# The delta stage of a state-space layer in 512-column pieces, with another split of its passes over the engines

## The chip, the cores and the metric

The kernel runs on one core of a Trainium2 chip. The metric is the device time of one execution in microseconds; smaller is better. Engines are called as in the profile: PE (TensorE), ACT (ScalarE), DVE (VectorE), POOL (GpSimd) and SP (SyncE, which issues most DMAs). Each has its own instruction queue, runs it in order and meets the others through semaphores.

## The reference, cut to what matters

The program is a state-space layer (norm, delta stage, scan, merge), then attention and a mixture of experts. Only the delta stage and its weights are touched. It works on 8 units (2 images times 4 branches of 64 channels), each 48x48 = 2304 positions long, with 128 inner channels:

```
x  = silu(conv3x3_depthwise(x @ in_W) + conv_b)         # 64 -> 128 channels
xs = [x0, x1, reversed x0, reversed x1]                 # x1 is x with rows and columns swapped
dts, B, C = split(einsum('bkdl,kcd->bkcl', xs, x_proj_W), [4, 16, 16])
delta = softplus(einsum('bkrl,kdr->bkdl', dts, dt_W) + dt_b)
# the scan then wants delta, delta * u, B and C for each of the 4 directions
```

## The kernel before, in words

`setup_phase` loads the weights with SP, multiplies dt_W with the first four rows of x_proj_W into one 128x128 matrix per direction (`w_eff`, L142), transposes the rest (`w_bc`, L147, L171) and makes the convolution's matrices `w_pair` and `w_one` (L166, L167). `norm_phase` writes the normalised input to `xn` in memory. Each phase ends for all engines before the next begins.

`delta_phase` loops over pairs of units (`Fori`, L389, L434, L500). A unit has 12 steps of 768 columns: 4 directions (0, 2, 1, 3) by 3 chunks. In a step:

- PE makes two 384-column products with `w_eff` in fp32 into `ps_a` (L376), one 384-column piece of B and C into `ps_b` (L380), and, on every second step, six matmuls of a convolution block of the *next* unit into `ps_c` (L361 with 128 rows, L362 with 64). Before the first unit all six of its blocks stand alone.
- ACT takes Abs and Relu of `ps_a` plus the bias (L415, L416), then Exp of minus Abs back into `ps_a` (L418). After three steps it switches its table and takes three logarithms (L402).
- DVE makes `dm` = (1 + e) - 1 (L477), copies `ps_b` out (L472), takes `ps_a` - `dm` (L448), and after three steps adds the logarithm (L455) and the Relu (L461), which gives delta.
- POOL multiplies delta with x (L518), turns x for directions 1 and 3 (L520), and makes `b_lo` (L508), the rest of B after its fp32r rounding `b_hi` (ACT, L407).
- SP stores `dd` (delta and delta*u together, L335), B and C (L320), `b_hi` and `b_lo` (L323) and x (L329), and loads images (L315) into `pad`, whose rows are 50 long, so that a row arrives in 192-byte runs.

`ps_a` has three buffers, and PE may start step n only when delta of step n-3 is written (`delta_done`, L373). Since DVE finishes three steps together, the engines work in bursts of three steps.

Of the kernel before, what the change touches and what calls it, by code (L numbers as in the profile page):

```python
# [22 lines left out]
K = 4  # L23
# [5 lines left out]
PAIRS = 2  # L29
SOFT = (4, 12)  # L30
# [41 lines left out]
def setup_phase(nc, P, w, keep):  # L72

    with ExitStack() as ctx:
        s = Space(nc, ctx, "setup")
        dts_rows = s.sb("dts_rows", [R, K, D])
        dtw_t = s.sb("dtw_t", [R, K, D])
        bc_rows = s.sb("bc_rows", [2 * N, K, D])
# [18 lines left out]
        loads.append((keep["dt_b"][:, :], w["dt_b"].rearrange("k d -> d k")))  # L97
# [13 lines left out]
        @block.sync  # L111
        def _(sp):
            for dst, src in loads:
                sp.dma_start(dst, src, allow_slow_non_contiguous=True).then_inc(loaded, 16)

        @block.gpsimd
        def _(pool):
            pool.memset(keep["ident"][:, :], 0.0).then_inc(ones_set, 1)
# [18 lines left out]
        @block.tensor  # L137
        def _(pe):
            pe.wait_ge(loaded, 16 * n_loads)

            for k in range(K):
                mm = pe.matmul(ps_w[:, k, 0:D], dts_rows[:, k, :], dtw_t[:, k, :], start=True, stop=True)  # L142
            mm.then_inc(weff_ps, 1)
            pe.wait_ge(ident_set, 1)
            pe.wait_ge(dve_done, 1)
            for k in range(K):
                mm = pe.transpose(ps_w[:, k, 256:256 + 2 * N], bc_rows[:, k, :], keep["ident"][0:2 * N, 0:2 * N])  # L147
            mm.then_inc(bc_ps, 1)

        @block.scalar  # L150
        def _(act):
            act.wait_ge(loaded, 16 * n_loads)
            act.activation(a_exp[:, :, :], a_log[:, :, :], ACT.Exp).then_inc(exp_done, 1)

        @block.vector
        def _(dve):
            dve.wait_ge(weff_ps, 1)
            dve.tensor_copy(keep["w_eff"][:, :, :], ps_w[:, :, 0:D]).then_inc(dve_done, 1)
            dve.wait_ge(exp_done, 1)
            dve.wait_ge(pool_set, 4)  # L160
            dve.tensor_scalar(keep["a_neg"][:, :, :], a_exp[:, :, :], -1.0, None, ALU.mult).then_inc(a_done, 1)

            for dy in range(3):
                for half in range(2):
                    p = slice(64 * half, 64 * half + 64)
                    dve.tensor_tensor(keep["w_pair"][p, dy, :], in_w2[p, :], conv_taps[p, :, 3 * dy + half], ALU.mult)  # L166
                dve.tensor_tensor(keep["w_one"][:, dy, :], in_w2[0:64, :], conv_taps[0:64, :, 3 * dy + 2], ALU.mult)  # L167
            dve.tensor_reduce(keep["d_sum"][:, :], ds4[:, :], AX.X, ALU.add)
            dve.wait_ge(bc_ps, 1)
            for r in range(2):  # L170
                dve.tensor_copy(keep["w_bc"][:, :, :].rearrange("d p (b r n) -> d r p b n", b=2, r=2)[:, r],  # L171
                                ps_w[:, 2 * r:2 * r + 2, 256:256 + 2 * N].rearrange("d p (b n) -> d p b n", b=2))
# [99 lines left out]
def delta_phase(nc, P, keep):  # L272
# [4 lines left out]
    with ExitStack() as ctx:  # L277
        s = Space(nc, ctx, "delta")

        pad = s.sb("pad", [128, 2, H + 2, W + 2])  # L280
        xs = [s.sb(f"xs{i}", [128, L]) for i in range(2)]
        xt = [s.sb(f"xt{i}", [128, L]) for i in range(2)]
        ring = lambda name: [s.sb(f"{name}{i}", [128, WC]) for i in range(3)]
        mag, pos, lg, dm = ring("mag"), ring("pos"), ring("lg"), ring("dm")
        dd = [s.sb(f"dd{i}", [128, 2, WC]) for i in range(3)]
        bc = [s.sb(f"bc{i}", [4 * N, L]) for i in range(2)]
        b_hi = [s.sb(f"b_hi{i}", [2 * N, L], F32R) for i in range(2)]
        b_lo = [s.sb(f"b_lo{i}", [2 * N, L], F32R) for i in range(2)]
        ps_a = [s.ps(f"ps_a{i}", [128, 2, 512]) for i in range(3)]
        ps_b = s.ps("ps_b", [4 * N, 512])  # L290
        ps_c = s.ps("ps_c", [128, 512])
        cleared, x_done, xt_done = s.sem("cleared"), s.sem("x_done"), s.sem("xt_done")
        img_here = [s.sem("img_here0"), s.sem("img_here1")]
        xs_out = [s.sem("xs_out0"), s.sem("xs_out1")]
        a_full, b_full, b_taken, c_full, c_taken = (s.sem(x) for x in ("a_full", "b_full", "b_taken", "c_full", "c_taken"))
        mag_done, ex_done, lg_done, hi_done = (s.sem(x) for x in ("mag_done", "ex_done", "lg_done", "hi_done"))
        dm_done, co_done, sm_done, delta_done = (s.sem(x) for x in ("dm_done", "co_done", "sm_done", "delta_done"))
        du_done, lo_done = s.sem("du_done"), s.sem("lo_done")
        dd_out = [s.sem(f"dd_out{i}") for i in range(3)]
        bc_out = [s.sem(f"bc_out{i}") for i in range(2)]  # L300
        block = ctx.enter_context(nc.Block())
        UP = U // 2
        Q = STEPS
        src = P["xn"].rearrange("b (r c) l -> (b r) c l", r=BR)
        halves = lambda x: x[:, :].rearrange("p (a b) -> p a b", a=2)
        order = [(p + 2 * r, c) for p in range(PAIRS) for r in range(2) for c in range(NCH)]
        bcd = P["bc"].rearrange("u (r p) b n l -> u p b r n l", p=PAIRS)
        cutd = P["cut"].rearrange("u (r p) a n l -> u p a r n l", p=PAIRS)

        @block.sync  # L310
        def _(sp):
            def load_image(n, k):
                img = src[n].rearrange("c (h w) -> c h w", h=H)
                for half in range(2):
                    sp.dma_start(pad[64 * half:64 * half + 64, k, 1:H + 1, 1 - half:W + 1 - half], img).then_inc(img_here[k], 16)  # L315

            def keep_bc(u, unit, p):
                sp.wait_ge(b_taken, unit * Q + 6 * p + 6 + 1)
                for b in range(2):
                    sp.dma_start(bcd[u, p, b], bc[p][32 * b:32 * b + 32, :]).then_inc(bc_out[p], 16)  # L320
                sp.wait_ge(lo_done, unit * PAIRS + p + 1)
                for a, cut in enumerate((b_hi, b_lo)):
                    sp.dma_start(cutd[u, p, a], cut[p][:, :].bitcast(F32)).then_inc(bc_out[p], 16)  # L323

            def pair(i, last):
                for k in range(2):
                    unit = i * 2 + k
                    sp.wait_ge(x_done, unit + 1)
                    sp.dma_start(P["xs"][i * 2 + k], xs[k][:, :]).then_inc(xs_out[k], 16)  # L329
                    if not last:  # L330
                        load_image(i * 2 + (k + 2), k)
                    for q, (d, c) in enumerate(order):
                        t = k * Q + q
# [1543 lines left out]
```

## Time and profile before

| | us |
|---|---|
| median of 3 runs (lowest to highest) | 6581.43 (6579.79 to 6591.75) |
| the profiled execution: its own time, its span | 6577.67, 6575.9 |
| setup and norm | 0 to 95.8 |
| delta stage, first to last engine instruction | 95.8 to 955.9 |
| first instruction of the scan | 988.75 |
| busy over the span: PE, DVE, POOL, ACT | 5383.8, 4385.1, 4109.4, 3873.2 |

Positions are microseconds from the start of the span. The share of busy time over the whole span says little of this change, since the scan (from 988.75) has two thirds of it; the stretch between 95.8 and 988.75 is what counts. TensorE's clock has two levels here, 1.2 GHz (0.50) and 2.4 GHz (1.00), and a stretch shows their mean.

### The profile page before, as it was taken

Reading aid. Unit: us, or ns where it says so; the run is one execution under the profiler, and the core shown is the slowest. Engines: PE = TensorE matmul, PEld = TensorE weight load, DVE = VectorE, ACT = ScalarE, POOL = GpSimd, SP = SyncE. Lnnn points to the kernel's source line nnn. Section 1 sums busy time; section 2 is a strip of 40 time slices with the busy share of each in tenths; the row PEclk is TensorE's granted clock in tenths of the full one; section 3 lists DMA queues with packets and bytes.
Section 4 is the critical chain, followed back from the end, with each engine's and each line's share of the span. In section 5 each row is a group of like instructions: output and inputs, shape, how many; then the busy total and the mean of one; then the engine's idle time right before and its main releaser. Section 6 shows DMA issues by size and latency. Waiting matters only on the chain. (4 is left out here: it accounts for less than half of the span.)

```text
span 6575.9 us, 86273 instructions
## 1 busy us (share of the span) xinstructions
PE 5383.8 (82%) x22548; PEld 3529.8 (54%) x22548; DVE 4385.1 (67%) x4337; ACT 3873.2 (59%) x7966; POOL 4109.4 (62%) x2729
## 2 busy tenths in 40 slices
PE   5767648999989899898998999955589999966994
PEld 2222215555555555555555555522269999944773
DVE  2455548999999999999999999967331211153332
ACT  2565557788778788778887888844532222232232
POOL 0233338999989999899998999942014444402441
PEclk7788879999999999999999999977789999975997
DMA  3344337777777777777777777765200000012213
GB/s 79 116 148 140 141 131 233 249 249 244 250 234 248 243 247 245 238 247 244 247 248 239 249 244 248 246 210 176 97 22 0 0 0 0 0 50 88 78 59 107
DMA packets 432423, 1073.25 MB, mean 163 GB/s; under 512 B 97545, under 2 KB 140586, under 8 KB 427386
## 3 DMA queue, kind: packets, MB, share of 16 engines
q1 hardware_dynamic: 420570, 1043.06, 48.9%
q0 software_dynamic: 7584, 20.72, 1.0%
q10 hardware_dynamic: 3840, 4.72, 0.3%
q8 instruction: 151, 2.47, 0.2%
q14 instruction: 278, 2.28, 0.1%
HBM read 883.38 MB, written 184.94 MB: 162 GB/s over the span
## 5 line engine op out<-in xcount | busy, mean ns | idle before, releaser
L852 POOL TENSOR_TENSOR scan_hc<-scan_h,scan_c_rep 128x768 f32<-128x768 f32 x1536 | 2745.3, 1828 | 282.1 <-PE scan_ps_y L683 220.2
L683 PE MATMUL scan_ps_y<-scan_hc,keep_ident 128*128 128x512 f32 (+1 forms) x6144 | 2221.9, 489 | 21.6 <-ACT scan_y L718 21.6
L817 DVE TENSOR_TENSOR_SCAN scan_h<-scan_da,scan_h,scan_ps_p 128x768 f32<-128x768 f32 x896 | 1573.4, 1795 | 0.0
L683 PEld LDWEIGHTS scan_ps_y<-scan_hc,keep_ident 128*128 128x128 f32 x6144 | 1070.2, 191 | 824.6 <-issue 740.6
L774 ACT ACTIVATE scan_da<-scan_dd,layer_a_neg 128x768 f32<-128x768 f32 x1344 | 1208.9, 925 | 195.9 <-DVE scan_h L817 190.3
L735 ACT ACTIVATE scan_warm<-scan_du_t 128x128 f32<-128x128 f32 x4032 | 1243.0, 388 | 2.5 <-PE scan_ps_p L674 1.9
L1194 POOL TENSOR_TENSOR attn_e_lo<-attn_e,attn_e_hi 128x384 fp32r<-128x384 f32 x432 | 438.2, 1014 | 773.1 <-DVE attn_e_hi L1185 773.1
L817 DVE TENSOR_TENSOR_SCAN scan_h<-scan_da,scan_ps_p 128x768 f32<-128x768 f32 x448 | 760.7, 1733 | 2.0 <-ACT scan_da L774 2.0
L796 DVE TENSOR_TENSOR scan_ps_p<-scan_ps_p,scan_dd 128x768 f32<-128x768 f32 x672 | 634.6, 944 | 137.2 <-PE scan_ps_p L666 135.7
L1185 DVE CAST attn_e_hi<-attn_e 128x384 fp32r<-128x384 f32 x432 | 165.3, 383 | 713.6 <-ACT attn_e L1173 713.6
L674 PE MATMUL scan_ps_p<-keep_ident,scan_warm 128*128 128x128 f32 x4032 | 580.5, 281 | 71.5 <-DVE scan_h L817 67.2
L1173 ACT ACTIVATE attn_e<-attn_ps_s 128x384 f32<-128x384 f32 x432 | 212.7, 492 | 692.4 <-PE attn_ps_s L69 692.4
L666 PE MATMUL scan_ps_p<-scan_cut,layer_b_sel 128*128 128x512 f32 x1344 | 434.7, 405 | 159.5 <-DVE scan_h L817 146.9
L674 PEld LDWEIGHTS scan_ps_p<-keep_ident,scan_warm 128*128 128x128 f32 x4032 | 444.9, 142 | 215.3 <-issue 138.1
L666 PEld LDWEIGHTS scan_ps_p<-scan_cut,layer_b_sel 128*128 128x128 f32 x1344 | 218.7, 190 | 341.2 <-DVE scan_h L817 301.6
L846 POOL TENSOR_TENSOR scan_bu<-scan_dd,scan_b_rep 128x768 f32<-128x768 f32 x192 | 350.3, 1825 | 0.0
L518 POOL TENSOR_TENSOR delta_dd<-delta_dd,delta_xs 128x768 f32<-128x768 f32 x48 | 86.1, 1810 | 402.7 <-DVE delta_dd L461 402.5
L67 PE MATMUL attn_ps_s<-f_hi,f_lo 128*128 x864 | 293.2, 339 | 2.1 <-DVE attn_t_lo L1181 2.1
L67 PE MATMUL attn_ps_o<-attn_e_hi,attn_t_lo 128*128 128x384 f32 x864 | 291.4, 337 | 3.8 <-POOL attn_e_lo L1194 3.8
L69 PE MATMUL attn_ps_s<-f_hi 128*128 x864 | 293.1, 339 | 0.0
L68 PE MATMUL attn_ps_s<-f_lo,f_hi 128*128 x864 | 291.6, 338 | 0.0
L69 PE MATMUL attn_ps_o<-attn_e_hi,attn_t_hi 128*128 128x384 f32 x864 | 291.5, 337 | 0.0
(279 smaller groups left out, 7483.2 us busy)
## 6 DMA issues: line engine op xcount, KB each, us to landing
scan_c_rep<-bc_dram SPq DMA_DIRECT2D x1536, 384.0 KB, 4.2
dd_dram<-delta_dd SPq DMA_DIRECT2D x96, 768.0 KB, 3.4
scan_dd<-dd_dram SPq DMA_DIRECT2D x96, 768.0 KB, 5.6
scan_b_rep<-bc_dram SPq DMA_DIRECT2D x192, 384.0 KB, 4.8
y_dram<-scan_y SPq DMA_DIRECT2D x96, 384.0 KB, 4.5
merge_y<-y_dram SPq DMA_DIRECT2D x32, 1152.0 KB, 10.6
delta_pad<-xn_dram SPq DMA_DIRECT2D x16, 576.0 KB, 27.3
xs_dram<-delta_xs SPq DMA_DIRECT2D x8, 1152.0 KB, 25.4
```

The source lines that it names most:

```text
L67: pe.matmul(out, wl, xh, start=start, stop=False)
L69: return pe.matmul(out, wh, xh, start=False, stop=stop)
L666: mm = pe.matmul(ps_p[place(t) % PR][:, lo:hi], keep["b_sel"][:, n, :], cut[st % 2][:, lo:hi], start=True, stop=True)
L674: mm = pe.transpose(ps_p[place(t) % PR][:, b * 128:b * 128 + 128], warm[w % WR][:, b, :], keep["ident"][:, :])
L683: mm = pe.matmul(ps_y[:, lo:hi], keep["ident"][:, :], hc[t % HR][:, lo:hi], start=n == 0, stop=n == N - 1)
L735: last = act.activation(warm[w % WR][:, b, :], du_t[st % 2][:, b * 128:b * 128 + 128], ACT.Identity, scale=du_t[st % 2][:, at:at + 1])
L774: act.activation(dst, dd[st % 2][:, 0, :], ACT.Exp, scale=keep["a_neg"][:, k, n:n + 1]).then_inc(ex_done, 1)
L796: dve.tensor_tensor(x, x, dd[st % 2][:, 1, :], ALU.mult).then_inc(mult_done, 1)
L817: dve.tensor_tensor_scan(view(h[n]), view(x), view(y), start, ALU.mult, ALU.add).then_inc(scan_done, 1)
L846: pool.tensor_tensor(bu[f % SR][:, :], dd[st % 2][:, 1, :], b_rep[f % SR][:, :], ALU.mult).then_inc(bu_done, 1)
L852: pool.tensor_tensor(hc[t % HR][:, :], h[t % N][:, :], c_rep[t % CR][:, :], ALU.mult).then_inc(hc_done, 1)
L1194: pool.tensor_tensor(e_lo[j % 4][:, :], e[j % 4][:, :], e_hi[j % 4][:, :].bitcast(F32), ALU.subtract).then_inc(lo_done, 1)
```

## The change

Everything up to the end of the norm keeps its order, but the weights differ: `w_eff` and `dt_b` are gone. Instead `w_dt` holds dt_W transposed as fp32r with the bias as one more row, and `w_dt_lo` what the rounding left of it; nine small loads (`late`) bring them, after the others.

The delta stage is written out without loops, as 16 rounds. A round is two directions of one unit, 0 and 2 (from `xs`) or 1 and 3 (from `xt`), 4608 columns in nine pieces of 512:

- `project` makes, for the next round, dts, B and C together (96 rows, 384 columns a block, six blocks a round). ACT rounds 40 rows into `cut` (and copies even blocks to `bc`), DVE writes the rest of the rounding into `cut` rows 64 to 103 (and copies odd blocks). Only then may PE start the next block.
- `expand` makes a piece of delta's argument out of `cut` with two fp32r matmuls (four in the piece across both directions).
- ACT takes Abs (without bias) and Exp into a second PSUM buffer `ps_e`; three logarithms of 1536 columns a round, in place in `du`.
- DVE makes `dm` in `du`, `ps_e` - `dm` in `de`, then max(`ps_a`, 0) + `de` in one pass; in the next round it adds the logarithm, 768 columns at a time, from SBUF to SBUF (`add_log`).
- POOL only multiplies with x and turns x.
- A convolution block is issued in halves of three matmuls. Its matrices are ordered by dx, so that images lie in `img` without a border inside a row (2304 columns in one run) and the outer taps have 47 of 48 columns. Three buffers of `xs` let it run up to two units ahead.
- SP stores delta and delta*u with two DMAs a chunk.

The stage's diff, cut to its core:

```diff
-        pad = s.sb("pad", [128, 2, H + 2, W + 2])
-        ps_a = [s.ps(f"ps_a{i}", [128, 2, 512]) for i in range(3)]
+        img = [s.sb(f"img{i}", [128, L + 2 * W]) for i in range(2)]
+        cut = [s.sb(f"cut{i}", [STACK, L], F32R) for i in range(2)]
+        de = [s.sb(f"de{i}", [128, 2 * L]) for i in range(2)]
+        du = [s.sb(f"du{i}", [128, 2 * L]) for i in range(2)]
+        ps_a = [s.ps(f"ps_a{i}", [128, PIECE]) for i in range(3)]
+        ps_e = [s.ps(f"ps_e{i}", [128, PIECE]) for i in range(3)]
+        SLOTS = (1, 2, 4, 5, 7, 8)
...
+            # SP
+            for g in range(G):
+                if g: store_dd(g - 1)
+                if g + 1 < G: store_bc(g + 1)
+                if p == 0 and u + 1 < U:
+                    store_xs(u + 1)
+                    if u + 3 < U: load_image(u + 3)
...
+            # PE
+            def project(g, b):
+                if m:
+                    pe.wait_ge(lo_done, m)
+                    pe.wait_ge(even_taken, (m + 1) // 2)
+                pe.matmul(ps_b[0:6 * N, 0:TT], keep["w_bc"][:, p, :], x[:, b * TT:b * TT + TT], ...).then_inc(b_full, 1)
+            def expand(g, i):
+                n = g * IG + i
+                if n >= 3: pe.wait_ge(v_done, n - 2)
+                for r, at, a, b in spans(i):
+                    pe.matmul(ps_a[n % 3][:, a:b], keep["w_dt"][:, d, :], cut[g % 2][:, at:at + b - a], ...)
+                    mm = pe.matmul(ps_a[n % 3][:, a:b], keep["w_dt_lo"][:, d, :], cut[g % 2][0:64, at:at + b - a], ...)
+                mm.then_inc(a_full, 1)
+            for t in range(TPI): convolve(0, t, 0, 6)
+            for t in range(3): convolve(1, t, 0, 6)
+            for b in range(TPI): project(0, b)
+            for g in range(G):
+                for i in range(IG):
+                    expand(g, i)
+                    if proj_block(g, i): project(*proj_block(g, i))
+                    if conv_block(g, i) and i % 3 < 2:
+                        convolve(*conv_block(g, i), 3 * (i % 3), 3 * (i % 3) + 3)
...
+            # ACT
+            def log(g, r):
+                act.wait_ge(co_done, IG * g + 3 * r + 3)
+                act.activation(x, x, ACT.Ln, bias=1.0).then_inc(ln_done, 1)
+            for g in range(G):
+                for i in range(IG):
+                    magnitude(n + 1)
+                    act.wait_ge(mag_done, n + 1)
+                    if n >= 3: act.wait_ge(co_done, n - 2)
+                    act.activation(ps_e[n % 3][:, :], mag[n % 3][:, :], ACT.Exp, scale=-1.0).then_inc(ex_done, 1)
+                    if i + 1 < IG and proj_block(g, i + 1): take_block(*proj_block(g, i + 1))
+                for r in range(LOGS): log(g, r)
+                if g % PAIRS == 0 and g // PAIRS + 1 < U: silu(g // PAIRS + 1)
...
+            # DVE
+            def add_log(g, j):
+                dve.wait_ge(ln_done, LOGS * g + j // 2 + 1)
+                dve.tensor_tensor(de[g % 2][:, at], de[g % 2][:, at], du[g % 2][:, at], ALU.add).then_inc(de_done, 1)
+                    if i == 0 and g >= 2: dve.wait_ge(dd_out[g % 2], 32 * CG * (g // 2))
+                    dve.wait_ge(ex_done, n + 1)
+                    dve.tensor_scalar(du[g % 2][:, at], ps_e[n % 3][:, :], 1.0, -1.0, ALU.add, ALU.add).then_inc(dm_done, 1)
+                    if i + 1 < IG and proj_block(g, i + 1): take_block(*proj_block(g, i + 1))
+                    dve.wait_ge(dm_done, n + 1)
+                    dve.tensor_tensor(de[g % 2][:, at], ps_e[n % 3][:, :], du[g % 2][:, at], ALU.subtract).then_inc(co_done, 1)
+                    if conv_block(g, i) and i % 3 == 1: take_conv(*conv_block(g, i))
+                    dve.wait_ge(co_done, n + 1)
+                    dve.scalar_tensor_tensor(de[g % 2][:, at], ps_a[n % 3][:, :], 0.0, de[g % 2][:, at], ALU.max, ALU.add).then_inc(v_done, 1)
+                    if g and 0 < i <= CG: add_log(g - 1, i - 1)
```

The order of DVE's instructions before, three steps of a unit (L477 makes `dm`, L472 copies `ps_b`, L448 corrects, L455 adds the logarithm, L461 the Relu):

```order
L477 TENSOR_SCALAR delta_dm<-delta_ps_a 128x768
L472 COPY delta_bc<-delta_ps_b 64x384
L448 TENSOR_TENSOR delta_ps_a<-delta_ps_a,delta_dm 128x2x384
L455 TENSOR_TENSOR delta_ps_a<-delta_ps_a,delta_lg 128x2x384 x2
L460 ISA
L461 TENSOR_TENSOR delta_dd<-delta_ps_a,delta_pos 128x768
L455 TENSOR_TENSOR delta_ps_a<-delta_ps_a,delta_lg 128x2x384
L461 TENSOR_TENSOR delta_dd<-delta_ps_a,delta_pos 128x768 x2
```

And now, pieces 1 to 3 of a round (L547 `dm`, L517 and L519 the next round's block, L551 the correction, L511 a convolution block, L555 max and add, L525 the logarithm of the round before):

```order
L547 TENSOR_SCALAR delta_du<-delta_ps_e 128x512
L517 COPY delta_bc<-delta_ps_b 96x384
L519 TENSOR_TENSOR delta_cut<-delta_ps_b,delta_cut 40x384
L551 TENSOR_TENSOR delta_de<-delta_ps_e,delta_du 128x512
L511 COPY delta_xs<-delta_ps_c 128x384
L555 SCALAR_TENSOR_TENSOR delta_de<-delta_ps_a,delta_de 128x512
L525 TENSOR_TENSOR delta_de<-delta_de,delta_du 128x768
L547 TENSOR_SCALAR delta_du<-delta_ps_e 128x512
L551 TENSOR_TENSOR delta_de<-delta_ps_e,delta_du 128x512
L555 SCALAR_TENSOR_TENSOR delta_de<-delta_ps_a,delta_de 128x512
L525 TENSOR_TENSOR delta_de<-delta_de,delta_du 128x768
```

The additions no longer come in a group after three steps: each `ps_a` buffer is given back within its own piece, and the logarithm is added a round later, out of SBUF.

ACT's order before, where it leaves one group of three steps for the next:

```order
L418 ACTIVATE delta_ps_a<-delta_mag 128x2x384
L402 ACT_TABLE_LOAD
L402 ACTIVATE delta_lg<-delta_dm 128x768 x3
L414 REGISTER_ALU
L415 ACTIVATE delta_mag<-delta_ps_a,layer_dt_b 128x768
L416 ACTIVATE delta_pos<-delta_ps_a,layer_dt_b 128x768
L417 REGISTER_ALU
L418 ACT_TABLE_LOAD
L418 ACTIVATE delta_ps_a<-delta_mag 128x2x384
```

And now, where it leaves one round for the next (L495 Exp, L480 the logarithms, L461 the silu of the next unit, after every second round, L475 Abs):

```order
L495 ACTIVATE delta_ps_e<-delta_mag 128x512
L480 ACT_TABLE_LOAD
L480 ACTIVATE delta_du<-delta_du 128x1536 x3
L461 ACT_TABLE_LOAD
L461 ACTIVATE delta_xs<-delta_xs,layer_conv_b 128x2304
L475 ACTIVATE delta_mag<-delta_ps_a 128x512
L495 ACT_TABLE_LOAD
L495 ACTIVATE delta_ps_e<-delta_mag 128x512
```

There were four such turns with two table loads each in a unit; now there are two, and the silu has moved into one of them.

PE's order now, pieces 1 to 3 of a round (L438 and L439 expand, L428 projects, L412 convolves):

```order
L438 MATMUL delta_ps_a<-delta_cut,layer_w_dt 128x512
L439 MATMUL delta_ps_a<-delta_cut,layer_w_dt_lo 128x512
L428 MATMUL delta_ps_b<-delta_xt,layer_w_bc 96x384
L412 MATMUL delta_ps_c<-delta_img,layer_w_one 128x8x47
L412 MATMUL delta_ps_c<-delta_img,layer_w_pair 128x8x47
L412 MATMUL delta_ps_c<-delta_img,layer_w_one 128x8x47
L438 MATMUL delta_ps_a<-delta_cut,layer_w_dt 128x512
L439 MATMUL delta_ps_a<-delta_cut,layer_w_dt_lo 128x512
L428 MATMUL delta_ps_b<-delta_xt,layer_w_bc 96x384
L438 MATMUL delta_ps_a<-delta_cut,layer_w_dt 128x512
L439 MATMUL delta_ps_a<-delta_cut,layer_w_dt_lo 128x512
```

Before, two fp32 matmuls of `w_eff` and one of `w_bc` (64 columns of weights) made a step, and a convolution block came whole after every second step.

## Rows read from the trace of the kernel before

**Rows 1.** The page: TensorE's clock in 40 slices, tenths of full speed.

```profile
PEclk7788879999999999999999999977789999975997
```

**Rows 2.** Stretches: us, busy us by engine, clock, DMA share, GB/s.

```profile
0.00:26.00 26.00, 2.68 (x12) 2.28 (x12) 4.28 (x14) 1.54 (x2) 8.85 (x15) 1.00 0.31 41
95.00:171.00 76.00, 57.16 (x72) 17.98 (x72) 7.01 (x6) 1.28 (x1) 0.00 (x0) 0.50 0.31 31
174.00:956.00 782.00, 513.59 (x1080) 184.02 (x1080) 409.74 (x522) 450.95 (x478) 283.95 (x120) 0.84 0.40 140
956.00:989.00 33.00, 0.00 (x0) 0.00 (x0) 0.25 (x1) 0.00 (x0) 0.00 (x0) 0.50 0.12 51
```

**Rows 3.** Timeline, stage start: start, length, engine, line, [idle before].

```profile
95.81 4.22 DVE L493 MEMSET delta_pad<- 128x5000 f32 x1 [8.03 <-issue]
110.59 1.65 PE L361 MATMUL delta_ps_c<-delta_pad,layer_w_pair 128*128 128x384 f32 x2 [30.59 <-DMA delta_pad<-xn_dram]
112.17 1.65 PE L362 MATMUL delta_ps_c<-delta_pad,layer_w_one 64*128 64x384 f32 x2
120.77 1.65 PE L361 MATMUL delta_ps_c<-delta_pad,layer_w_pair 128*128 128x384 f32 x2 [0.65 <-DVE delta_xs L442]
```

**Rows 4.** Timeline, inside the delta stage, a group of three steps.

```profile
508.83 0.89 ACT L415 ACTIVATE delta_mag<-delta_ps_a,layer_dt_b 128x768 f32<-128x768 f32 x1
509.61 0.89 ACT L416 ACTIVATE delta_pos<-delta_ps_a,layer_dt_b 128x768 f32<-128x768 f32 x1
510.54 0.81 ACT L418 ACTIVATE delta_ps_a<-delta_mag 128x768 f32<-128x768 f32 x1
517.68 1.82 DVE L455 TENSOR_TENSOR delta_ps_a<-delta_ps_a,delta_lg 128x768 f32<-128x768 f32 x2
520.41 2.93 PE L376 MATMUL delta_ps_a<-delta_xt,layer_w_eff 128*128 128x384 f32 x4 [4.10 <-DVE delta_dd L461]
```

**Rows 5.** Delta stage by line: busy us, mean ns, idle before, releaser.

```profile
L477 DVE TENSOR_SCALAR delta_dm<-delta_ps_a 128x768 f32<-128x768 f32 x96 | 91.9, 958 | 228.9 <-ACT delta_ps_a L418 228.9
L448 DVE TENSOR_TENSOR delta_ps_a<-delta_ps_a,delta_dm 128x768 f32<-128x768 f32 x96 | 91.3, 951 | 0.0
L415 ACT ACTIVATE delta_mag<-delta_ps_a,layer_dt_b 128x768 f32<-128x768 f32 x96 | 86.0, 896 | 317.4 <-PE delta_ps_a L376 317.3
L418 ACT ACTIVATE delta_ps_a<-delta_mag 128x768 f32<-128x768 f32 x96 | 78.2, 814 | 2.4
L402 ACT ACTIVATE delta_lg<-delta_dm 128x768 f32<-128x768 f32 x96 | 73.9, 832 | 0.4
L402 ACT ACT_TABLE_LOAD x32 | 41.1, 1283 | 0.6
L397 ACT ACTIVATE delta_xs<-delta_xs,layer_conv_b 128x2304 f32<-128x2304 f32 x8 | 17.7, 2215 | 75.3 <-DVE delta_xs L442 75.2
L518 POOL TENSOR_TENSOR delta_dd<-delta_dd,delta_xs 128x768 f32<-128x768 f32 x48 | 86.1, 1810 | 402.7 <-DVE delta_dd L461 402.5
```

**Rows 6.** Timeline, two convolution matmuls at the upper clock level.

```profile
501.40 0.91 PE L361 MATMUL delta_ps_c<-delta_pad,layer_w_pair 128*128 128x384 f32 x2
502.24 0.91 PE L362 MATMUL delta_ps_c<-delta_pad,layer_w_one 64*128 64x384 f32 x2
```

**Rows 7.** Stretch in which TensorE only convolves, at the lower clock level.

```profile
233.00:240.00 7.00, 7.00 (x11) 2.15 (x9) 1.23 (x2) 0.00 (x0) 0.00 (x0) 0.52 0.00 0
```

**Rows 8.** Timeline of the scan: a fp32r pair of 512 and 256 columns.

```profile
2001.27 0.62 PE L666 MATMUL scan_ps_p<-scan_cut,layer_b_sel 128*128 128x512 f32 x2 [0.33 <-DVE scan_h L817]
```

**Rows 9.** Whole span, VectorE with 512 columns out of PSUM.

```profile
L1778 DVE TENSOR_TENSOR moe_h_lo<-moe_ps_t,moe_h_hi 128x512 fp32r<-128x512 f32 x79 | 54.7, 692 | 51.2 <-ACT moe_h_hi L1750 51.2
```

**Rows 10.** A VectorE operation with two SBUF inputs, ns min/median/max.

```profile
L953 DVE TENSOR_TENSOR merge_yy<-merge_yc,merge_sd x48: 548/558/1917, 4372.9 to 4600.3; 128x384 f32<-128x384 f32 x48
```

**Rows 11.** SP's longest wait (us, times, longest), and its stretch.

```profile
SPq L349 <- DMA cut_dram<-delta_b_lo: 27.0, 1, 27.0
...
957.00:984.00 27.00, 0.00 (x0) 0.00 (x0) 0.00 (x0) 0.00 (x0) 0.00 (x0) 0.50 0.13 53
```

More of the change, by code:

```diff
@@ L29 @@
 PAIRS = 2
+STACK = 104
+PIECE = 512
 SOFT = (4, 12)
@@ L139, in _ @@
             pe.wait_ge(loaded, 16 * n_loads)
+            pe.wait_ge(ident_set, 1)
             for k in range(K):
[L142 to L147, printed above, removed]
+                mm = pe.transpose(ps_w[:, k, 0:R + 2 * N], x_rows[:, k, :], keep["ident"][0:R + 2 * N, 0:R + 2 * N])
             mm.then_inc(bc_ps, 1)
@@ L294, in delta_phase @@
[L294 to L299, printed above, removed]
@@ L317, in keep_bc @@
-            def keep_bc(u, unit, p):
-                sp.wait_ge(b_taken, unit * Q + 6 * p + 6 + 1)
-                for b in range(2):
[L320 to L333, printed above, removed]
-                        sp.wait_ge(du_done, unit * Q + q + 2)
-                        sp.dma_start(P["dd"][i * 2 + k, d, c], dd[t % 3][:, :, :]).then_inc(dd_out[t % 3], 16)
-                        if q == 8:
-                            keep_bc(i * 2 + k, unit, 0)
-                    keep_bc(i * 2 + k, unit, 1)
@@ L386, in _ @@
-            pe.wait_ge(img_here[0], 32)
-            for t in range(TPI):
-                convolve(0, 0, t)
-            with pe.Fori(0, UP - 1) as i:
-                pair(i, False)
-            pair(UP - 1, True)
+                RB = TT // W
+                if first == 0:
+                    if t == 0:
+                        pe.wait_ge(img_here[unit % 2], 32 * (unit // 2) + 32)
+                    pe.wait_ge(c_taken, unit * TPI + t)
+                taps = [(dx, one) for dx in (1, 0, 2) for one in range(2)]
@@ new lines, in convolve @@
+                for n in range(first, last):
+                    dx, one = taps[n]
+                    a, b = max(0, 1 - dx), min(W, W + 1 - dx)
+                    if one:
+                        lhs, rows, x = keep["w_one"][:, dx, :], slice(r0 + 2, r0 + 2 + RB), iv[0:64]
+                    else:
+                        lhs, rows, x = keep["w_pair"][:, dx, :], slice(r0, r0 + RB), iv
+                    mm = pe.matmul(ov[:, :, a:b], lhs, x[:, rows, a + dx - 1:b + dx - 1], start=n == 0, stop=n == 5)
@@ new lines, in magnitude @@
+            def magnitude(n):
+                act.wait_ge(a_full, n + 1)
+                act.activation(mag[n % 3][:, :], ps_a[n % 3][:, :], ACT.Abs).then_inc(mag_done, 1)
+            def log(g, r):
+                act.wait_ge(co_done, IG * g + 3 * r + 3)
+                x = du[g % 2][:, r * 3 * PIECE:(r + 1) * 3 * PIECE]
+                act.activation(x, x, ACT.Ln, bias=1.0).then_inc(ln_done, 1)
+            silu(0)
+            act.wait_ge(ones_set, 2)
+            for b in range(TPI):
+                take_block(0, b)
@@ new lines, in _ @@
+            for k in range(2):
+                dve.memset(img[k][:, :], 0.0)
+            for k in range(2):
+                last = dve.memset(cut[k][32:64, :].bitcast(F32), 1.0)
+                last.then_inc(ones_set, 1)
+            last = dve.memset(mag[0][:, 0:1], 0.0)
+            last.then_inc(cleared, 1)
+            for t in range(TPI):
+                take_conv(0, t)
+            for t in range(3):
+                take_conv(1, t)
+            for b in range(TPI):
+                take_block(0, b)
@@ L527, in scan_phase @@
+            turn(0)
+            for g in range(G):
+                for j in range(CG):
+                    drive(g, j)
+                if g % PAIRS == 0 and g // PAIRS + 1 < U:
+                    turn(g // PAIRS + 1)
 def scan_phase(nc, P, keep):
```

376 lines of the change are left out of this document (193 added, 183 removed).

## Prediction

> **What bounds the kernel now.** I read four views in this order: the page, to see where TensorE's clock is low; busy time by stretch, to find the stage's length and whether any engine fills it; the timeline of the stage, for what hands over to what; and the groups by line, for durations.
>
> The page shows the clock at 7 to 8 tenths up to the seventh slice and at 9 after it [rows 1]: the delta stage is where TensorE is not steadily busy. From 174 to 956 us no engine fills its time: PE 514 of 782 us, ACT 451, DVE 410, POOL 284, DMA 0.40 [rows 2]. So the stage is bound by waiting on one another, about 98 us a unit. The timeline shows the mechanism: after a group of three steps PE waits 4.10 us for `delta_dd` [rows 4], because all three `ps_a` buffers come free only at the group's end. DVE waited 228.9 us in front of L477 for ACT's Exp, ACT 317.3 us in front of L415 for PE [rows 5]: a ring in which each engine waits for the next. After each such gap PE's clock has fallen, so the next group starts slower.
>
> Two pieces lie outside that ring. From 110.59 PE convolves unit 0 alone, at clock 0.50, a block taking 120.77 - 110.59 = 10.18 us [rows 2, 3]. And the end: SP waits 27.0 us for the last `cut` store, in which 0.13 of the DMA engines move 53 GB/s [rows 11]. That is two engines of 16, some 26.5 GB/s each. B, C and `cut` go out with two rows in front (one for each direction) and use only two engines.
>
> **The change, part by part.** Positions count from the span's start. Call one round's time P.
>
> *Setup.* Loads go from one transposed copy of dt_W to eight, which wait for their buffer. The transposed one delays SP most already. Setup and the way to the norm take 26 us [rows 2]; the late loads queue behind the others and feed one copy and one subtraction. Bounds: -2 (three loads fewer in front) to +8; I take +2.
>
> *Start of the stage.* One memset of 5000 columns costs 4.22 us [rows 3], 0.845 ns a column; now 2 x 2400 + 2 x 2304 columns, 8.0 us. Images come in one run a row; 2.4 MB at the full rate, 16 x 26.5 = 424 GB/s, is about 6 us for both, and I allow 6 to the first matmul (10.5 before, from 100.03 to 110.59). PE starts at 95.8 + 8 + 6 = 110. It now convolves nine blocks alone, all of unit 0 and half of unit 1: 9 x 10.18 = 92, at the lower level as six do now. Then six projections, each through PE (1.6), ACT (two copies of 384, 1.0), DVE (0.6): about 3.3 us, 20 in all. The first piece adds 3. The rounds begin at 225 (against 174). Bounds of the convolutions: 9 x (6 x 0.84 + 0.7) = 52 at the upper level [rows 6] to 92. Only-convolving stretches stay at the lower level even with PE busy 7.00 of 7.00 us [rows 7], so I take 92.
>
> *DVE in a round.* A 512-column pass out of PSUM lasts 0.69 us [rows 9]. Two passes of 768 end 1.82 us after the first began, each 0.95, so a pass follows another after 0.87, 0.08 less than it lasts [rows 4]. So a pass costs 0.61, or 0.72 where its successor needs its result. Of 27 passes nine are of the latter kind: 9 x 0.72 + 18 x 0.61 = 17.5. Six additions of 768 columns: 6 x 0.87 = 5.2. Twelve operations of 384 columns (six `cut`, three `bc`, three convolution blocks): 0.47 each, 5.6. Sum 28.3.
>
> *The turn of a round.* After the last piece's correction, ACT still has a logarithm of 1536 columns, Abs, a table load and Exp before DVE has work again. The logarithm takes 0.83 + 0.64 = 1.47, Abs 0.90 - 0.22 = 0.68, the load 1.28, Exp 0.81 - 0.22 = 0.59 [rows 5]: 4.0, of which DVE's last pass covers 0.7. DVE idles 3.3. Every second time silu and its load come between, 2.2 + 1.3: 6.8. Mean 5.0. The earlier two logarithms are hidden, since DVE is then two to three pieces behind ACT. ACT's own sum (18 short activations at 0.5 to 0.6, nine copies, 4.2 of logarithms, loads, silu) is about 22, not the bound.
>
> *PE in a round.* A fp32 matmul of 384 columns costs 0.84 at the upper level [rows 6], 1.58 at the lower [rows 3]. 18 in convolutions and 6 projections: 20.2. A fp32r pair of 512 and 256 columns ends after 0.62 [rows 8]; a piece's two of 512 I put at 0.6, nine pieces 5.6. Sum 26 at the upper level, 47 at the lower. PE fits beside DVE only at the upper level. It idles at each turn: 3 to 7 us, and a 4.10 us gap is followed now by matmuls at the lower level, four records in 2.93 us [rows 4]. At the lower level 6 to 7 us of work stretch by half of that; in the middle of a round PE (8.7 us for three pieces) has only 0.7 of slack against DVE (9.4), so most of it is passed on: +3.2. So P = 28.3 + 5.0 + 3.2 = 36.5.
>
> *DMA in a round.* Four stores of 288 KB on two engines: 1.18 MB / 53 = 22.2 us. Delta and delta*u: 12 x 384 KB over 16 engines, 11.1 us on each. Images and x: 2.8. The two engines need 36.1 a round, at the rate of [rows 11]. That is as long as P, with about one round of buffering (`de`, `du`, `bc`, `cut` in two copies). Two limits this close to each other disturb one another; I add 0.8. P = 37.3. The ends: 33.3 (DVE and turns alone) and 47 to 48 (PE at the lower level).
>
> *POOL.* 6 x 1.81 = 10.9 [rows 5] and half a turn of x, well inside.
>
> *A rule that speaks against the change.* `add_log` has both inputs in SBUF, and POOL's product is released by it. In the merge such a DVE operation, 0.55 us alone, takes up to 1.92 us [rows 10], as long as a POOL product beside it. Here the product starts 0.05 after an addition ends and lasts 1.81; the next addition comes after a piece of three passes, 2.05 us at least, so they just miss. In the sum the rule costs nothing but the tail. The Trainium skill, page SBUF — State Buffer, section "SBUF: two separate sides", says that VectorE with two SBUF inputs and a GpSimd operation that reads SBUF lock each other out for a whole instruction. By that rule the merge row is a lock, and a product that came 0.2 us later here would stop DVE for its length; that is rival D.
>
> *The end.* Rounds 1 to 13 take 13 x 37.3 = 485. The last three have no convolution: two of 28.3 - 1.4 + 3.3 = 30, and one of 21 without blocks and turn. These outrun the two DMA engines, +6. Then six additions and products in turn, 6 x (0.87 + 1.81) = 16, and a store: 17. The 27 us of the last `cut` store go, since it is issued a round earlier. Scan starts at 225 + 485 + 81 + 6 + 17 + 2 = 816, against 988.75. Gain 173.
>
> The scan and all behind it are the same instructions on the same data in memory: 0. The profiled execution took 6577.67: 6577.67 - 173 = 6405; it lay 3.8 under the median, so 6408 for the median.
>
> **Rivals.**
> A, the forecast: 6408, own range 6365 to 6455 (P between 34.5 and 41).
>
> B, PE's clock rises early: 40 less at the start (52 instead of 92), and P falls to what the two DMA engines need, 36.1: 13 x 1.2 = 16 less. 6352; where their stores also overlap better than I think, P = 34 and 6325. For it: PE's share of a round is higher than now. Against it: [rows 3, 7].
>
> C, PE's clock stays low within rounds: half of the convolution matmuls have 64 rows, and convolving alone doesn't raise the clock [rows 7]. P = 48, 13 x 10.7 = 139 more: 6547. Against it: mixed work between 174 and 956 reached 0.84 [rows 2].
>
> D, `add_log` and the products meet: each of six additions in a round waits up to 1.3 us, P + 8, 104 more: 6512.
>
> E, slower than before: PE at the lower level and the turns not overlapped at all. A projection needs the previous block back from ACT and DVE, and PE, in order, holds convolution and expansion behind it. Then 47 and 7 to 9 add: P = 55, 13 x 17.7 = 230 more: 6638. It decides for slower from P = 50.6, where 173 is used up (173 / 13 = 13.3 above 37.3). The like of it is seen now: PE's 4.10 us wait [rows 4]. Against it: expansions run up to three pieces ahead.
>
> F, the change doesn't do what it says: its cuts are real in the instruction order, but DMA queues at the two engines could push P to 50 if other traffic shares them; then about 6575, no change.
>
> **How the numbers follow.** A 0.60, B 0.13, C 0.10, D 0.07, E 0.08, F 0.02. The likeliest gives 6408. The range 6340 to 6505 holds A, most of B and the mild half of C and D, 0.80 together. A difference of 0.2% (13 us) is about what can be told from no change. Faster by more: A to D, 0.90. Within it: F, 0.02. Slower: E, 0.08.
>
> **What the profile after would show.** Scan's first instruction near 816. Rounds of 37 us, seen in the distance from one silu to the next: 75 (before 98). Nine convolution blocks alone at clock 0.50 till about 202. In a round DVE idle 3 to 4 us at each turn and 7 at every second, before the first `dm`, released by ACT; L525 at 0.95 us mean, not 1.5 (D); POOL under half busy. The two DMA engines busy nearly throughout (DMA share never near 0), no 27 us wait at the end. The forecast is wrong if PE's clock is at 0.5 to 0.6 within the rounds (C, E), if DVE waits at a round's start for `dd_out` (DMA is the bound), or if the rounds start later than 240.

## The result

| | us, median (lowest to highest) | ratio to before, 95% interval |
|---|---|---|
| kernel before, the same session | 6580.61 | 1 |
| kernel after | 6645.5 (6642.26 to 6663.32) | 1.0101 [1.0079, 1.0123] |

The kernel became slower by 1%, where 6408 with a range of 6340 to 6505 was forecast. In the profiled execution (span 6640.5 us) the scan starts at 1062.12 instead of 988.75 us; what follows takes 5578 us against 5587 before. So the loss lies in the delta stage.

The page after: TensorE's clock, to be read beside [rows 1].

```profile
PEclk7555557999999999999999999987789999975897
```

Stretches of the kernel after (us, busy us of PE, weight loads, DVE, ACT, POOL, clock, DMA share, GB/s), as in [rows 2]: the nine convolution blocks that stand alone, and the middle of the rounds.

```profile
115.40:205.40 90.00, 84.69 (x108) 26.96 (x108) 4.46 (x8) 2.21 (x1) 4.07 (x1) 0.50 0.14 36
250.00:600.00 350.00, 307.61 (x431) 108.61 (x430) 185.10 (x282) 138.43 (x207) 75.67 (x38) 0.51 0.32 117
```

The clock's record has 0.50 without a break from 86 to 567 us. In [rows 2] the clock between 174 and 956 us was 0.84. Now it is 0.51, and PE is busy 308 of 350 us, while DVE is busy 185, ACT 138 and POOL 76. PE has become the bound. From one silu to the next, two rounds, the trace has 111.8 us: P = 55.9, where 37.3 was forecast.

TensorE's timeline in three pieces of a round (start, length, engine, line, count, [idle before <- releaser]), at the lower level.

```profile
577.69 1.62 PE L412 MATMUL delta_ps_c<-delta_img,layer_w_pair 128*128 128x376 f32 x2
...
582.50 1.62 PE L412 MATMUL delta_ps_c<-delta_img,layer_w_one 64*128 64x376 f32 x2
584.05 1.62 PE L412 MATMUL delta_ps_c<-delta_img,layer_w_pair 128*128 128x376 f32 x2
585.61 1.62 PE L412 MATMUL delta_ps_c<-delta_img,layer_w_one 64*128 64x376 f32 x2
587.15 0.79 PE L438 MATMUL delta_ps_a<-delta_cut,layer_w_dt 104*128 104x512 f32 x1
587.88 0.79 PE L439 MATMUL delta_ps_a<-delta_cut,layer_w_dt_lo 64*128 64x512 f32 x1
588.60 1.59 PE L428 MATMUL delta_ps_b<-delta_xt,layer_w_bc 128*96 128x384 f32 x2
...
593.13 1.65 PE L412 MATMUL delta_ps_c<-delta_img,layer_w_pair 128*128 128x384 f32 x2 [1.78 <-DVE delta_xs L511]
```

A convolution matmul follows the last one after 1.55 us, a pair of expanding matmuls (587.15 to 588.60) takes 1.45, and once in three pieces PE waits until VectorE has copied the convolution block out (L511), 1.8 us on average and 2.6 at most between 250 and 600 us. Groups of the kernel after between 90 and 1080 us (busy us, mean ns, idle before and its releaser); ScalarE and VectorE wait where they did in [rows 5], and longer.

```profile
L412 PE MATMUL delta_ps_c<-delta_img,layer_w_one 64*128 64x376 f32 (+1 forms) x288 | 230.1, 900 | 0.0
...
L439 PE MATMUL delta_ps_a<-delta_cut,layer_w_dt_lo 64*128 64x512 f32 (+1 forms) x160 | 118.1, 738 | 0.0
...
L547 DVE TENSOR_SCALAR delta_du<-delta_ps_e 128x512 f32<-128x512 f32 x144 | 99.0, 688 | 322.9 <-ACT delta_ps_e L495 322.9
...
L475 ACT ACTIVATE delta_mag<-delta_ps_a 128x512 f32<-128x512 f32 x144 | 85.7, 595 | 433.7 <-PE delta_ps_a L439 433.6
```

The waits between 250 and 600 us (total, times, longest); the last is PE's wait for silu, once a unit:

```profile
ACT delta_mag L475 <- PE delta_ps_a L439: 197.7, 53, 8.0
DVE delta_du L547 <- ACT delta_ps_e L495: 151.6, 38, 8.3
...
PE delta_ps_c L412 <- DVE delta_xs L511: 35.0, 19, 2.6
...
PE delta_ps_b L428 <- ACT delta_xs L461: 7.4, 3, 2.5
```

The tail is as forecast, near enough: the last additions and products take 20.6 us to the scan's first instruction (17 forecast), and SP's 27 us wait [rows 11] is gone.

```profile
1041.54 11.71 DVE L525 TENSOR_TENSOR delta_de<-delta_de,delta_du 128x768 f32<-128x768 f32 x6
1042.57 14.10 POOL L575 TENSOR_TENSOR delta_du<-delta_de,delta_xt 128x768 f32<-128x768 f32 x6 [3.15 <-DVE delta_de L525]
...
1062.12 1.50 DVE L887 MEMSET scan_cut<- 128x768 f32 x2 [8.87 <-PEq L286]
```

### The profile page after: what moved, and what is told of

Same layout as the page of the kernel before. It is cut to its first block and busy times, and to the rows that moved or that the text cites. A ratio compares the mean times of both kernels' runs of the same rounds, so it can differ in the third digit from the quotient of the medians.

```text
span 6640.5 us, 85890 instructions
## 1 busy us (share of the span) xinstructions
PE 5592.6 (84%) x22476; PEld 3598.1 (54%) x22476; DVE 4455.1 (67%) x4543; ACT 3776.0 (57%) x8015; POOL 4033.4 (61%) x2715
## 5 line engine op out<-in xcount | busy, mean ns | idle before, releaser
L575 POOL TENSOR_TENSOR delta_du<-delta_de,delta_xs 128x768 f32<-128x768 f32 x48 | 86.8, 1808 | 415.4 <-DVE delta_de L525 415.4
L475 ACT ACTIVATE delta_mag<-delta_ps_a 128x512 f32<-128x512 f32 x144 | 85.7, 595 | 433.7 <-PE delta_ps_a L439 433.6
L412 PE MATMUL delta_ps_c<-delta_img,layer_w_pair 128*128 128x376 f32 (+1 forms) x288 | 232.3, 910 | 108.0 <-DVE delta_xs L511 75.3
L547 DVE TENSOR_SCALAR delta_du<-delta_ps_e 128x512 f32<-128x512 f32 x144 | 99.0, 688 | 322.9 <-ACT delta_ps_e L495 322.9
```

The source lines that it names most:

```text
L412: mm = pe.matmul(ov[:, :, a:b], lhs, x[:, rows, a + dx - 1:b + dx - 1], start=n == 0, stop=n == 5)
```

## The experiments

There were two theories at first. **C**: PE at the lower clock level sets the round, because half-array matmuls (64 rows) hold the clock down. **S**: the waits of the engines on one another, in a ring, set the round, and the clock is low because PE waits. The differences between runs below are between their medians; each ratio is to the kernel before, measured beside that run.

**1. `a1_rows128`**: w_one padded to 128 rows with zeros.

```
-"w_one": [DM, 3, D]                     +"w_one": [128, 3, D]     # rows 64 to 127 are 0
-x = iv[0:64]                            +x = iv
```

> The kernel after, with the third tap of each convolution column (w_one) padded from 64 to 128 partitions by zero weights, so that all six matmuls of a convolution block use the whole array; the number of matmuls, their columns and all waits stay. Theory C (the half-array matmuls keep the granted clock at its lower level, and PE at that level sets the round): the granted clock of the delta stage rises from 0.50 to near 1, the nine blocks before the rounds take about 52 us instead of 92, a round falls from 55.9 to 37-41 us, the time to about 6380-6460. Theory S (the serial waits of the ring set the round, and the clock is low because PE waits): the clock stays low in the rounds, which keep 54-56 us, and the time stays within 0.3% of 6645 (the start may win up to 40 us if the clock rises there alone: 6600-6650).

Measured: 6412.3, ratio 0.9748 [0.9731, 0.9764]. The scan starts at 822.1 us, a round takes 39.8 us on average. The nine blocks' stretch and the rounds:

```profile
115.40:205.40 90.00, 69.31 (x169) 34.22 (x170) 24.00 (x42) 17.18 (x30) 4.10 (x1) 0.82 0.19 53
250.00:600.00 350.00, 270.36 (x595) 130.46 (x595) 255.66 (x396) 191.20 (x287) 114.98 (x57) 0.78 0.47 173
```

TensorE's timeline, the first two blocks:

```profile
118.48 1.49 PE L413 MATMUL delta_ps_c<-delta_img,layer_w_one 128*128 128x384 f32 x2
119.76 1.46 PE L413 MATMUL delta_ps_c<-delta_img,layer_w_pair 128*128 128x376 f32 x2
...
124.81 0.81 PE L413 MATMUL delta_ps_c<-delta_img,layer_w_one 128*128 128x384 f32 x2
125.46 0.80 PE L413 MATMUL delta_ps_c<-delta_img,layer_w_pair 128*128 128x376 f32 x2
126.09 0.80 PE L413 MATMUL delta_ps_c<-delta_img,layer_w_one 128*128 128x376 f32 x2
```

Theory S is out: 233 us came back with the same instructions and waits in the same order. But the rows show a second thing. From 118.48 to 119.76 a matmul of 384 columns takes 1.28 us at the lower level; in [rows 3] and in the kernel after it took 1.57 to 1.58. At the upper level it is 0.65 for 384 columns (124.81 to 125.46) and 0.63 for 376, against 0.84 for 384 in [rows 6]. The padded matmul is shorter at either level.

**2. `a2_allrows128`**: as 1, and the expanding matmuls padded (`w_dt` from 104, `w_dt_lo` from 64, `cut` from 104 rows to 128).

> As a1_rows128, and the expanding matmuls too are padded to 128 partitions (104 and 64 rows before), with zero weights. Theory C: if the convolution's rows alone do not lift the clock, this does: 6380-6460; if they do, this equals a1_rows128 within 10 us. Theory S: as a1_rows128, no change from 6645.

Measured: 6390.8, 0.9716 [0.9700, 0.9732]; round 38.5. That is another 21 us, where 10 at most were expected.

**3. `b1_rows128`**: the kernel before with the padding of 1.

> The kernel before, with the same padding of w_one to 128 partitions. Theory C: the kernel before loses a part of its stage to the lower level too (95 to 174 us, where the convolution runs alone); there it gains, 20 to 50 us: 6530-6560. Theory S: it stays at 6580, within 5 us.

Measured: 6525.6, 0.9921 [0.9905, 0.9938]: the tuned kernel had the same loss in small. With the padding on both sides the redesign gains 0.9748 / 0.9921 = 0.9826, 113 us; the forecast sign was right for a kernel without this loss.

**4. `a3_no_lo`**:

```
-mm = pe.matmul(ps_a, keep["w_dt_lo"], cut[0:64], start=False, stop=True)
```

> The kernel after without the matmul of the low part of the step's weights (w_dt_lo); the step is less exact. Theory C: PE sheds nine matmuls a round, at 0.74 us each and two for the split piece some 7.4 us, so at an unchanged level the round falls from 55.9 to about 48.5 and the time by 110-125 us, to 6520-6535 (less late rounds that VectorE bounds). Theory S (chain of waits through one piece): the matmul lies on the chain from the projection to Abs once a piece too, so it would fall also, but where a round waits for the convolution's single buffer by less: 20-60 us, 6585-6625.

Measured: 6499.1, 0.9878 [0.9861, 0.9894]; round 44.4, 11.5 less and not 7.4, and the clock rose to 0.65 between 250 and 600 us. The time lies below theory C's 6520. PE sets the round, but its price per matmul was not understood yet.

**5. `c1_take_early`**: the copy of a convolution block moved forward.

```
-if conv_block(g, i) and i % 3 == 1: take_conv(...)     # between passes 2 and 3
+if conv_block(g, i) and i % 3 == 0: take_conv(...)     # after pass 3, ahead of add_log
```

> The kernel after, with VectorE's copy of a convolution block out of PSUM moved: at the end of the first piece of three, ahead of the addition of a logarithm, instead of between the second and third pass of the second piece. The matmuls keep their 64-row forms, so the clock stays low. In the kernel after PE waits for this copy once in three pieces (68.2 us over 37 waits between 250 and 1000 us, the long ones 1.8 to 2.6 us, 18.0 us for three pieces). Theory C+W (clock and waits add): with PE bound at the lower level, each wait that goes shortens the three pieces by it, 5.4 to 7.8 us a round, so the round is 48-50 us and the time 6535-6570. Rival (the wait only moves to the next expanding matmul, which waits for VectorE too): within 15 us of 6645.

Measured: 6588.7, 1.0012 [1.0003, 1.0022], 57 us less than the kernel after; round 51.3. Two stretches, one that lies within the rounds of one unit and one over several units, and the waits of the latter:

```profile
400.00:478.00 78.00, 78.00 (x110) 27.79 (x109) 48.31 (x73) 29.56 (x50) 24.04 (x12) 0.50 0.35 134
250.00:600.00 350.00, 327.53 (x471) 115.87 (x471) 205.82 (x309) 157.40 (x232) 78.32 (x40) 0.53 0.36 131
```

```profile
PE delta_ps_b L428 <- ACT delta_xs L461: 21.5, 4, 6.3
```

Between two silus PE is busy 78.00 of 78 us at clock 0.50 and waits for nothing. Over 350 us it idles 22.5, nearly all of it for silu, once a unit: a round of 51.3 is 48.0 of work (327.53 / 350) and 3.3 idle. The kernel after's 55.9 is, in the same way, 49.1 of work and 6.8 idle, and 5.6 of these are waits for the copy (35.0 us in 350) and 1.2 for silu (7.4). The waits add to the work as long as PE is the bound, as theory C+W (the clock and the waits add) said, but 4.6 us a round were won and not 5.4 to 7.8, and 6588.7 lies above its 6535 to 6570. The 5.6 are gone; the wait for silu grew from 1.2 to 3.3, and the expectation had left it out.

**6. `c2_take_early_128`**: 2 and 5 together.

> a2_allrows128 with the same earlier copy. There PE waits 91.1 us over 33 waits between 250 and 690 us, 2.7 us in each three pieces of 12. If that wait sets the round there: 38.5 falls by up to 8 to 31-33 us, or to 36 where the stores on two DMA engines (36.1 us a round by the forecast's sum) bound it: 6270-6310 without, 6340-6360 with that bound. If VectorE and ScalarE's chain sets it (VectorE waits 102 us for the exponential there): 6370-6390.

Measured: 6371.0, 0.9680 [0.9664, 0.9696]; round 37.3. The 20 us won lie at the edge of the last case expected (VectorE's and ScalarE's chain sets the round, 6370 to 6390), and so PE's waits for the copy (91.1 us between 250 and 690 us in run 2) were for the most part not what bound it. VectorE also waits for the stores at the start of some rounds:

```profile
DVE delta_du L550 <- DMA dd_dram<-delta_du: 29.0, 4, 8.5
```

**7. `c4_take_early_128_split`**: as 6, the stores of bc and cut one for each direction.

```
-sp.dma_start(bcd[u, p, b], bc[64*b : 64*b+32])           # 32 rows, two runs in front
+for r in range(2): sp.dma_start(bcd[u, p, b, r], bc[64*b+16*r : 64*b+16*r+16])
```

> c2_take_early_128 with the four stores of bc and cut of a round split into eight, one for each direction, 16 rows of 9 KB each, so that more DMA engines share them. If the stores bound the round of c2 (36 us), this is 20 to 60 us faster than c2; if not, it is equal to it within 5 us, or slower by the four more issues (some 3 us a round on SP, which waits anyway).

Measured: 6349.7, 0.9646 [0.9629, 0.9662]; round 35.9, and the wait of 6 is gone. The four stores that used two DMA engines cost 1.4 us a round here, 21 us in all.

**8. `c3_pool_adds_128`**: 2 with the logarithm added by GpSimd ahead of its product (`pool.tensor_tensor(de, de, du, ALU.add)` in `drive`, `add_log` gone).

> a2_allrows128, with the logarithm added by GpSimd ahead of its product, as the kernel before has it, instead of by VectorE between its passes. VectorE sheds six additions of 0.95 us a round, GpSimd takes six of about 1.8 us, its busy time goes from 11 to 22 us of a round of 38.5. Theory C+W (PE's work and its wait for the copy set the round): the copy comes up to 0.95 us earlier in some pieces, and the tail after the last piece is 6 x 0.9 us longer: -40 to +10 us, 6350-6400. Rival L (an addition on GpSimd holds VectorE's two-operand passes off): VectorE's passes beside it take longer, the time rises by 20 to 60 us: 6410-6450.

Measured: 6382.2, 0.9701 [0.9683, 0.9719]: not told apart from 2. No sign of rival L.

**9. `d2_best_pool_adds`**: 7 with the same edit.

> c4_take_early_128_split with the logarithm added by GpSimd ahead of its product. In c4 VectorE is busy 29.2 us of a round of 35.9 and waits 6 us for ScalarE's turn between rounds; PE has slack. If VectorE sets the round there, its six additions (5.7 us) go: 30-32 us a round, 6265-6300 with 5 us more tail. If ScalarE's logarithms, table loads and the ring's handing over set it, or a busier GpSimd slows VectorE's two-operand passes: 34-37 us, 6330-6375.

Measured: 6305.7, 0.9581 [0.9565, 0.9597], the fastest version, 44 us ahead of 7; round 32.1. The same edit changed nothing in run 8. Between 8 and 9 lie the earlier copy and the split stores; no run tells which of them makes the addition's engine matter. Stretches of 7 and of 9:

```profile
250.00:600.00 350.00, 231.19 (x662) 122.67 (x663) 283.84 (x437) 212.53 (x321) 123.74 (x63) 0.91 0.66 194
```

```profile
250.00:600.00 350.00, 251.99 (x734) 138.63 (x732) 266.26 (x429) 237.10 (x363) 257.33 (x137) 0.88 0.73 216
```

In 350 us run 7 gets through 9.7 rounds with VectorE busy 284, and run 9 through 10.9 with VectorE busy 266; GpSimd, with 257, is still inside.

**10. `d1_expand128_only`**: 2 without the padding of w_one.

> The kernel after, with only the expanding matmuls padded to 128 partitions (104 and 64 before); w_one keeps its 64 rows. Tells whose half-array matmuls hold the clock down. If it is w_one's (one in two of the convolution): the clock stays at 0.50 in the rounds, the nine blocks ahead of them keep 10 us each, and the time stays within 15 us of 6645. If any more rows help (rows summed over all matmuls): the clock rises in part, the round falls to 40-50 us, 6430-6560; the nine blocks alone stay slow, since nothing in them changed.

Measured: 6520.1, 0.9901 [0.9885, 0.9918]; the nine blocks stay at 0.50, the round falls to 44.4. More full matmuls help here too. This fits idle rows, but also another reading: padding removes a *change* of the row count from one matmul to the next. The timeline of 1 (1.28 against 1.57) speaks for the change. Three runs tell them apart: theory **M**, a matmul pays where its row count differs from its predecessor's; theory **R**, idle rows.

**11. `e1_order`**: the kernel after, one line.

```
-taps = [(dx, one) for dx in (1, 0, 2) for one in range(2)]
+taps = [(dx, one) for one in range(2) for dx in (1, 0, 2)]
```

> The kernel after with the six matmuls of a convolution block in another order: the three with 128 rows first, then the three with 64, instead of in turn. Same matmuls, same rows, same waits. Theory M (a matmul pays about 0.3 us at the lower level wherever the row count differs from its predecessor's, and the gaps this makes keep the clock down): four of six switches of a block alone go, so a block of the first nine takes 10.1 - 4 x 0.3 = 8.9 us or less (6 where the clock rises); in three pieces four of some 12 switches go, at least 1.2 us of 18, so 6590 if the clock stays low and 6480-6560 if it rises in part. Theory R (the idle rows keep the clock down): the clock stays at 0.50 throughout as in the kernel after; the time is 6590-6645.

Measured: 6461.0, 0.9826 [0.9810, 0.9842], 184 us less than the kernel after with the same matmuls, and 19 us below theory M's own range (6480 to 6560): the switches that go count, and the clock rises more than it said. The blocks alone:

```profile
117.57 4.15 PE L412 MATMUL delta_ps_c<-delta_img,layer_w_pair 128*128 128x384 f32 x6 [32.62 <-DMA delta_img<-xn_dram]
121.65 2.64 PE L412 MATMUL delta_ps_c<-delta_img,layer_w_one 64*128 64x384 f32 x6
124.94 2.17 PE L412 MATMUL delta_ps_c<-delta_img,layer_w_pair 128*128 128x384 f32 x6 [0.65 <-DVE delta_xs L511]
127.04 2.17 PE L412 MATMUL delta_ps_c<-delta_img,layer_w_one 64*128 64x384 f32 x6
129.87 2.17 PE L412 MATMUL delta_ps_c<-delta_img,layer_w_pair 128*128 128x384 f32 x6 [0.65 <-DVE delta_xs L511]
```

The second block starts at 124.94 and the third at 129.87: 4.93 us a block, against 10.07 in the kernel after (115.41 to 125.48), and three 64-row matmuls last 2.17 us like the three of 128 rows. The stretches:

```profile
115.40:205.40 90.00, 71.72 (x164) 32.56 (x164) 20.36 (x35) 14.59 (x25) 4.08 (x1) 0.81 0.19 53
250.00:600.00 350.00, 284.51 (x531) 126.14 (x531) 232.64 (x357) 174.22 (x260) 101.54 (x51) 0.67 0.43 158
```

**12. `e2_order_expand128`**: 10 with the order of 11.

> d1_expand128_only (expanding matmuls padded to 128 rows, w_one kept at 64) with the convolution in the same new order. Theory M: of the switches only two in three pieces are left (into and out of the three 64-row matmuls), so it comes close to a2_allrows128 (6391): 6400-6440. Theory R (the share of idle rows counts, the order does not): as d1_expand128_only, 6505-6530.

Measured: 6401.5, 0.9737 [0.9721, 0.9754]: 119 us less than 10, and within 11 us of 2, with w_one at 64 rows.

**13. `e3_before_order`**: the kernel before with that order.

> The kernel before with its convolution in the new order (three 128-row matmuls, then three of 64 rows). Theory M: most of what padding gave it (b1_rows128, 6526) comes without padding: 6530-6550. Theory R: 6575-6585, no change.

Measured: 6531.2, 0.9936 [0.9919, 0.9953], close to the padded 3. M's direction holds in all three runs (11 gained even more), R's in none: changes of the row count cost time, and no cost of idle rows shows. The Trainium skill, page TensorEngine Tiling (Array Packing), section "Key Properties", says that changing the tiling mode, not just the tile, drains TensorE. Runs 11 to 13 agree with it, if a matmul of 64 rows and one of 128 are two modes.

No run tries 104 rows apart, but the timelines bear on it. Here is the first pair of expanding matmuls with what follows it, at the lower level, first of the kernel after (104 and 64 rows), then of run 2 (128 and 128):

```profile
222.35 1.20 PE L438 MATMUL delta_ps_a<-delta_cut,layer_w_dt 104*128 104x512 f32 x1
223.49 0.79 PE L439 MATMUL delta_ps_a<-delta_cut,layer_w_dt_lo 64*128 64x512 f32 x1
224.21 1.01 PE L412 MATMUL delta_ps_c<-delta_img,layer_w_pair 128*128 128x384 f32 x1
```

```profile
182.50 1.20 PE L440 MATMUL delta_ps_a<-delta_cut,layer_w_dt 128*128 128x512 f32 x1
183.50 0.63 PE L441 MATMUL delta_ps_a<-delta_cut,layer_w_dt_lo 128*128 128x512 f32 x1
183.92 1.30 PE L414 MATMUL delta_ps_c<-delta_img,layer_w_pair 128*128 128x384 f32 x2
```

In front of both stands a projection of 128 rows. Up to the matmul behind the pair the first takes 1.86 us and the second 1.42. The 0.44 between them are no more than the changes to 64 rows and back cost at about 0.3 each, so a change from 128 to 104 seems to cost nothing.

## Why the prediction was wrong, point by point

Right: the rounds begin at 222.4 us (225 forecast), after nine blocks at 10.07 us and six projections at 3.2; from the last silu (945.3), where the 13 rounds with a convolution end, the scan starts after 117 us (104 forecast for the last rounds, DMA and tail); the scan and what follows did not change; in the rounds `add_log` takes 0.95 us, so rival D was none (between 300 and 1000 us):

```profile
L525 DVE TENSOR_TENSOR delta_de<-delta_de,delta_du 128x768 f32<-128x768 f32 x81 | 76.8, 949 | 0.0
```

It is longer only in the tail, where the longest of the six takes 2.56 us with a product beside it, as the operation of [rows 10] did.

The step that failed is *PE in a round*, and in it one choice: "26 at the upper level, 47 at the lower", with "PE fits beside DVE only at the upper level", and the sum built on the upper one. PE stayed at the lower and took 49.1. With the waits, the 13 rounds from 222.4 to 945.3 us took 723 us where 13 x 37.3 = 485 were forecast, 238 of the 246 us by which the scan starts late against the forecast (1062 against 816). The prediction's own sign for this, PE's clock at 0.5 to 0.6 within the rounds, is there (0.51). Its other two signs are not: VectorE waits for no store, and the rounds don't start late. How the choice went wrong:

- I held [rows 2], "mixed work reached 0.84", against rival C. But that mix had the 128-row `w_eff` products in it, which the change takes out; the new mix changes its row count at nearly every matmul, like the convolution alone, for which [rows 7] showed the lower level at full busy time. The rows that resembled the new work were the ones I argued away.
- I took 0.84 and 1.58 us [rows 3, 6] for the price of a convolution matmul. They hold a change of the row count each; without it the price is 0.65 and 1.28 (run 1). So the bound for the nine blocks at the upper level, 52, was too high as well: run 11 takes 4.93 a block, 44.
- I priced a pair of expanding matmuls at 0.6 from a pair of the scan [rows 8] in which both have 128 rows. With 104 and 64 rows it is 1.45 at the lower level. The sum for the lower level, 47, came near the 49.1 all the same, since its convolution price, 1.58, held the change already.

Of the rivals E came about, given 0.08: 6638 forecast, 6645 measured, P = 55 forecast (47 and 7 to 9), 55.9 measured (49.1 and 6.8). The size was right and the place of the waits only in part: not the projection's way through ACT and DVE, but the copy of the one `ps_c` buffer is four fifths of them (5.6 of 6.8). C had the same cause without the waits; run 5, in which the wait for the copy is gone, has 51.3, with 3.3 for silu still in it. Both rest on the level, and I held both at 0.18 together.

With TensorE repaired the rest of the model comes close. Run 7, which also has the earlier copy and the split stores, has a round of 35.9, where 28.3 + 5.0 + 3.2 = 36.5 stood before the surcharge for DMA, and VectorE is busy for 29.1 of it (283.84 / 350), where 28.3 stood. The surcharge, 0.8, was 1.4 (runs 6 and 7); it had no run behind it. Run 1 at 6412 against 6408 is in part luck: its rounds begin at 177 us instead of 225 and take 39.8 instead of 37.3.

Open: why changes of the row count keep the granted clock at its lower level. The runs show that both go together; they do not show what the clock reacts to.

## What to carry to other kernels

Put matmuls with the same number of rows next to each other, or pad the short ones with zero weights: a change of the row count costs 0.2 to 0.3 us here, and with one at nearly every matmul the clock stayed at 1.2 GHz for 480 us (86 to 567). Take the price and the clock of a new mix from rows in which the same shapes follow each other, not from an average over other work. And when a change removes an engine's slack, look for the single buffer that this engine fills and another empties: a wait there costs nothing while the engine has slack, and added 5.6 us to each round here.

## What the runs showed of the hardware

- A matmul of 64 rows behind one of 128 (or the reverse), fp32, 384 columns: 1.57 us at the lower level (kernel after) and 0.84 at the upper [rows 6]. Between neighbours of 128 rows (run 1): 1.28 at the lower, 0.65 at the upper. Three of 64 rows in turn last 2.17 us at the upper level, as three of 128 rows do (run 11).
- Rows padded with zeros did not keep the clock down: in the stretch of the nine blocks it was 0.82 with them (run 1) and 0.81 with the new order and no padding (run 11).
- PE was busy 78.00 of 78 us at granted clock 0.50 (run 5): full busy time in the profile did not raise the level by itself.
